# Graph attention layer: the own and row-aligned values are weighted and summed by GpSimd instead of VectorE

## The chip, the core and the metric

One core of a Trainium2 chip runs the kernel. The time is device microseconds of one execution. The engines of the core are TensorE (PE in the profile, PEld its weight loads), VectorE (DVE), ScalarE (ACT), GpSimd (POOL) and SyncE (SP); each works through its own instructions in the order in which they were written, and they wait for each other only by semaphores.

## What is computed

The reference is one layer of a graph network over 4096 nodes with 256 features, 8 heads of 32, all in float32; adj is a sparse matrix of 0 and 1.

```python
mask = adj.astype(jnp.float32) + jnp.eye(n, dtype=jnp.float32)
q = (h @ Wq.T + bq).reshape(n, N_HEADS, D_K)      # k, v in the same way
scores = jnp.einsum('nhd,mhd->hnm', q, k) / jnp.sqrt(jnp.float32(D_K))
scores = jnp.where(mask[None, :, :] == 0, jnp.float32(-1000000000.0), scores)
attn = jax.nn.softmax(scores, axis=-1)
ctx = jnp.einsum('hnm,mhd->nhd', attn, v).reshape(n, D_MODEL)
attn_out = ctx @ Wo.T + bo
h1 = _layer_norm(h + attn_out, ln1_g, ln1_b)
ff = jax.nn.relu(h1 @ W1.T + b1) @ W2.T + b2
return _layer_norm(h1 + ff, ln2_g, ln2_b)
```

## The kernel before

The kernel uses the sparsity. A first stage (up to about 100 us) projects keys, values and queries of all nodes and stores them as tables in device memory. VectorE searches each row of adj for its ones (`find_dve`, FIND_INDEX8 on L485), which gives lists of neighbours. A row of nodes sits on each of the 128 partitions; a tile is 128 nodes.

For each tile, keys and values come from three places: the node's own row (one plain load), the first one or two neighbours of each node (the row-aligned ones, gathered straight to the node's partition by GpSimd with indirect DMAs, L932), and the rest, the edges, packed into units of 128 and gathered by GpSimd (L940 for keys and values, L944 for queries). Own and aligned values are multiplied by their probabilities and added up elementwise; the edges are multiplied by theirs and then summed per node by TensorE with a one-hot matrix (`sum_pe`, L814), which adds the own sum in the same accumulation (L815).

The tiles after the first stage go in 19 steps, numbered 0 to 18 here. Steps 0 to 9 and 17, 18 hold two tiles, steps 10 to 16 one tile. Two tiles have 2 own slots each (own and one aligned), or 3 each in steps 6 to 9; a single tile has 3 own slots, or 4 in steps 14 and 15. Tile 0, with the most edges, is spread in pieces over steps 2 to 14. Two to four steps make a group of four tiles, and the dense part of a group (output projection L990, layer norm, feed-forward L1009 and L1021, second layer norm) is spread over the steps of the next group. The first step of a group is called place 0, the next place 1. The groups begin at steps 0, 2, 4, 6, 8, 10, 14 and 17.

The order of a step q on each engine is written out by hand. On VectorE: edge scores, own scores (`own_scores_dve`, whose reduction waits for `own_weighted` of the step before, since it overwrites the probabilities), mask and maximum, then the indices of the next step's edges (`cols_dve`, which lets GpSimd gather them), `norm_probs_dve` (ends with the own probabilities, semaphore `own_probs`), a search of a row tile for the step after next (one FIND_INDEX8 over 4105 elements for the two-tile steps), `edge_below_dve` (L651, after which ScalarE takes the exponential, L877), `own_sum_dve`, `edge_weight_dve` (L680, L683), a second search, the lists, and at place 0 the statistics of the second layer norm (L1075). On GpSimd: aligned gathers of the next step, four small operations of the first layer norm (`post_pool_rstd`) at place 0, edge gathers of the next step, at steps 2 to 8 two gathers for tile 0, then either gain and final of the output (L1102, L1106) at place 1 or the second `post_pool_rstd` at place 0. In steps 0 and 1, stores of query tiles (`store_q`, L1388) stand between them. TensorE's `sum_pe` waits for three semaphores: `edge_weighted`, `own_sum` and `own_weighted`. Behind it stand the dense matmuls of the step, and in steps 0 and 1 the last query projections. The aligned and edge gathers that reuse the buffers of step q wait for its `sum_pe` (semaphore `acc_ps`).

Of the kernel before, what the change touches and what calls it, by code (L numbers as in the profile page):

```python
# [5 lines left out]
ALU = mybir.AluOpType  # L6
# [6 lines left out]
P = 128  # L13
N = 4096
D = 256
HEADS = 8
DK = D // HEADS
# [97 lines left out]
def total(value, upto):  # L115

    return sum(value(q) for q in STEPS[:upto])
# [12 lines left out]
def build(nc, xT, adj, wqkvT, bq, bk, bqkv, woT, w1T, w2T, cols, g2, be2, out):  # L130
    with ExitStack() as ctx:
# [197 lines left out]
        own_probs = sem("own_probs")  # L329
# [70 lines left out]
        def wait(eng, s, value):  # L400
            if not isinstance(value, int) or value > 0:
                eng.wait_ge(s, value)
# [20 lines left out]
        def own_slots(q, ti):  # L423
            return slots[q.par][:, ti * q.own:(ti + 1) * q.own, :]
# [4 lines left out]
        def score_tiles(q):  # L429
            return scores[:, 0:q.T * q.S * HEADS].rearrange("p (t s h) -> p t s h", t=q.T, h=HEADS)  # L430

        def unit_scores(q, lo, hi):

            all_units = score_tiles(q)[:, :, 1:, :]
            if q.nu == 1:
                return all_units[:, :, lo:hi, :]
            return all_units[:, 0, :, :].rearrange("p (u r) h -> p u r h", r=q.room)[:, :, lo:hi, :]
# [213 lines left out]
            nc.vector.tensor_tensor(p_edge[:, 0:q.U, :], s_edge[:, 0:q.U, :], tr_out(q)[:, :, 0:HEADS], ALU.subtract  # L651
                                    ).then_inc(edge_below, 1)

        def own_sum_dve(dve, q):

            dve.wait_ge(own_probs, q.b + 1)
            for ti in range(q.T):
                v = own_slots(q, ti)[:, :, D:].rearrange("p s (h d) -> p s h d", d=DK)
                if q.nu == 1:
                    p = score_tiles(q)[:, ti, 0:q.own, :]  # L660
                    last = nc.vector.tensor_tensor(v, v, p.unsqueeze(3).to_broadcast([P, q.own, HEADS, DK]), ALU.mult)
                else:
                    p = score_tiles(q)[:, ti, 0:1, :]
                    last = nc.vector.tensor_tensor(v[:, 0:1], v[:, 0:1], p.unsqueeze(3).to_broadcast([P, 1, HEADS, DK]), ALU.mult)
                    if q.A:
                        p = unit_scores(q, 0, 1)[:, :, 0, :]
                        last = nc.vector.tensor_tensor(v[:, 1:], v[:, 1:], p.unsqueeze(3).to_broadcast([P, q.U, HEADS, DK]), ALU.mult)
            last.then_inc(own_weighted, 1)
            dve.wait_ge(own_weighted, q.b + 1)
            done = total(lambda p: p.own - 1, q.b)  # L670
            v = slots[q.par][:, 0:q.T * q.own, D:].rearrange("p (t s) d -> p t s d", s=q.own)
            for a in range(1, q.own):
                wait(dve, own_sum, done + a - 1)
                nc.vector.tensor_tensor(v[:, :, 0, :], v[:, :, 0, :], v[:, :, a, :], ALU.add).then_inc(own_sum, 1)  # L674

        def edge_weight_dve(dve, q):
            dve.wait_ge(edge_exp, q.b + 1)

# [217 lines left out]
        def ctx0_act(act):  # L896
            act.wait_ge(psum0, 2 * PIECES0 + 2)
            for k in range(KC):
                last = nc.scalar.activation(ctxT[:, k, TILE0.j * P:(TILE0.j + 1) * P], ps[:, ACC, k * 2 * P:(k * 2 + 1) * P], ACT.Identity,
                                            bias=bias_v[:, k:k + 1])  # L900
            last.then_inc(ctx0_ready, 1)

# [445 lines left out]
        def _(pool):  # L1350
# [49 lines left out]
            for q in STEPS:  # L1400
# [10 lines left out]
                    store_q(p)  # L1411
                if soon:
                    gather_edges(pool, soon)
                if 0 <= i - GATHER0 < PIECES0:
                    gather_edges(pool, TILE0, (2 * (i - GATHER0), 2 * (i - GATHER0) + 1))
                for gap in range(3, 5):
# [241 lines left out]
        def _(dve):  # L1658
# [43 lines left out]
            for q in STEPS:  # L1702
# [28 lines left out]
                if i == WEIGHTS0:  # L1731
                    edge_below0_dve(dve)
                edge_below_dve(dve, q)
                own_sum_dve(dve, q)
                edge_weight_dve(dve, q)
                if i == WEIGHTS0:
                    weight0_dve(dve, 0)
# [60 lines left out]
```

## Time and profile before

| | |
|---|---|
| median of 3 runs | 682.92 us |
| lowest, highest | 676.41, 685.6 us |
| the profiled execution's own time | 665.67 us |
| its span in the trace | 663.7 us |
| mean granted clock of TensorE | 0.903 |
| busy: TensorE, VectorE, GpSimd, ScalarE | 80%, 72%, 36%, 26% |

Busy shares are means over the span. The chain of waits is followed back from the last instruction, at each step to what released it, and tells which engine's work the end hung on at each time. A timeline row gives the start and the duration in us, and in brackets the idle time of that engine before it with what ended it. An indirect DMA on POOL is the time in which GpSimd issues it, not its transfer.

### The profile page before, as it was taken

To read this page: it belongs to the slowest core of one execution; us is meant where nothing else is said; L and a number is where in the kernel's file an instruction comes from. 1 tells how busy PE (TensorE), PEld (TensorE's weight loads), DVE (VectorE), ACT (ScalarE), POOL (GpSimd) and SP (SyncE) were. 2 spreads that over 40 slices of the span, in tenths; PEclk is the share of its full clock that TensorE was granted. 3 is DMA by queue.
4 is the path that set the end of the run, shared out by engine and by line. 5 is a ranking of instruction groups with operands and counts; after the bars stand their busy time and mean duration, and the time that the engine had idled before them with its cause. 6 is when DMAs were issued, how large, how long until landed. Compare 5 with 4: busy or idle time off the path is not lost.

```text
span 663.7 us, 7651 instructions
## 1 busy us (share of the span) xinstructions
PE 530.3 (80%) x2434; PEld 420.0 (63%) x2434; DVE 478.3 (72%) x1210; ACT 170.1 (26%) x357; POOL 238.9 (36%) x368
## 2 busy tenths in 40 slices
PE   6979679886797988789889785587858598989791
PEld 5868567775466748646775672366745368577680
DVE  1659687898885997999789798989985996412000
ACT  1111122212321341242224133111213213521610
POOL 5100033634331465446452434324351524122222
PEclk9989769989698999899789998678978889999896
DMA  9974689999886689686645527066672753020100
GB/s 332 409 302 161 230 309 327 406 347 339 325 285 229 217 317 336 200 341 239 253 134 207 206 58 259 19 244 244 223 236 66 262 182 110 18 64 0 33 16 19
DMA packets 39211, 141.08 MB, mean 213 GB/s; under 512 B 4856, under 2 KB 15352, under 8 KB 35072
## 3 DMA queue, kind: packets, MB, share of 16 engines
q1 hardware_dynamic: 24176, 94.90, 38.7%
q0 software_dynamic: 13328, 43.55, 19.2%
q10 hardware_dynamic: 1664, 2.11, 1.0%
q8 instruction: 21, 0.34, 0.2%
q14 instruction: 22, 0.18, 0.1%
HBM read 123.74 MB, written 16.80 MB: 212 GB/s over the span
## 4 chain that ended last, share of the span: by engine, by line
PE 43%; DVE 33%; issue 8%; DMA 7%; ACT 5%; POOL 3%; DVEq 0%; POOLq 0%; ACTq 0%
PE ps L1009 12%; PE ps L1021 10%; DVE found L485 8%; PE ps L990 4%; PE ps L980 3%; DMA adj_buf<-in_adj 3%; DVE stats L1075 2%; PE ps L1555 2%; PE ps L814 2%; PE ps L1573 2%; DMA work<-q_table,row_of 2%; PE ps L777 2%; DVE slots L674 2%; PE ps L815 1%; ACT early L1065 1%
## 5 line engine op out<-in xcount | busy, mean ns | idle before, releaser
L485 DVE FIND_INDEX8 found<-ones,adj_buf 128x8 uint32<-128x4105 int32 (+19 forms) x54 | 145.2, 2689 | 0.0
L1009 PE MATMUL ps<-xT_all,w 128*128 128x512 f32 (+1 forms) x288 | 129.5, 597 | 11.1 <-ACT xT_all L1055 10.0
L1021 PE MATMUL ps<-w,xT_all 128*128 128x256 f32 x512 | 121.9, 393 | 3.6 <-ACT xT_all L1055 2.7
L1021 PEld LDWEIGHTS ps<-w,xT_all 128*128 128x128 f32 x512 | 98.8, 198 | 17.7 <-ACT xT_all L1055 3.6
L1009 PEld LDWEIGHTS ps<-xT_all,w 128*128 128x128 f32 x288 | 57.2, 208 | 60.4 <-issue 45.4
L940 POOL DMA_INDIRECT slots<-kv_table,col_of x54 | 54.2, 1004 | 63.8 <-DVE col_of L558 52.2
L1075 DVE BATCH_NORM_STATS2 stats<-ps 128x6 f32<-128x256 f32 x64 | 22.9, 419 | 64.0 <-PE ps L980 64.0
L1555 PE MATMUL ps<-early,xT_all 128*128 128x256 f32 x256 | 63.6, 413 | 6.1 <-DMA early<-in_wqkvT 6.0
L1055 ACT ACTIVATE xT_all<-ps,col_table 128x512 f32<-128x512 f32 (+1 forms) x72 | 45.4, 642 | 71.5 <-PE ps L1009 65.7
L1555 PEld LDWEIGHTS ps<-early,xT_all 128*128 128x128 f32 x256 | 53.3, 210 | 14.8 <-DMA early<-in_wqkvT 6.0
L814 PE MATMUL ps<-work,slots 128*128 128x128 f32 x160 | 34.8, 327 | 28.8 <-DVE slots L683 28.8
L1093 POOL TENSOR_TENSOR rstd<-mv,eps_col 128x4 f32<-128x4 f32 (+1 forms) x18 | 5.4, 298 | 131.6 <-DVE mv L1081 131.6
L932 POOL DMA_INDIRECT slots<-kv_table,found x32 | 34.1, 1065 | 49.4 <-issue 23.2
L814 PEld LDWEIGHTS ps<-work,slots 128*128 128x128 f32 x160 | 28.1, 233 | 33.2 <-DVE slots L683 33.1
L990 PE MATMUL ps<-wo,xT_all 128*128 128x256 f32 x128 | 37.0, 415 | 14.3 <-issue 11.1
L944 POOL DMA_INDIRECT work<-q_table,row_of x40 | 39.2, 980 | 12.2 <-issue 12.2
L884 ACT ACTIVATE xT_all<-ps,col_table 128x256 f32<-128x256 f32 (+1 forms) x38 | 14.5, 431 | 109.4 <-PE ps L815 109.4
L1102 POOL TENSOR_TENSOR early<-early,row_g 128x1024 f32<-128x1024 f32 (+1 forms) x9 | 19.0, 2109 | 49.6 <-DVE slots L683 43.9
L1573 PE MATMUL ps<-early,xT_all 128*128 128x256 f32 x128 | 35.3, 401 | 0.0
L777 PE MATMUL ps<-idx_all,work 128*128 128x9 f32 (+1 forms) x80 | 12.7, 270 | 28.2 <-DVE work L539 28.2
L990 PEld LDWEIGHTS ps<-wo,xT_all 128*128 128x128 f32 x128 | 23.7, 206 | 16.9 <-issue 14.9
L777 PEld LDWEIGHTS ps<-idx_all,work 128*128 128x128 f32 x80 | 11.4, 206 | 32.6 <-DVE work L539 32.6
(160 smaller groups left out, 885.1 us busy)
## 6 DMA issues: line engine op xcount, KB each, us to landing
adj_buf<-in_adj SPq DMA_DIRECT2D x32, 2048.0 KB
xT_all<-in_xT SPq DMA_DIRECT2D x15, 512.0 KB, 22.0
kv_table<-slots POOLq DMA_DIRECT2D x7, 1024.0 KB, 5.0
slots<-kv_table SPq DMA_DIRECT2D x12, 512.0 KB
q_table<-slots POOLq DMA_DIRECT2D x16, 256.0 KB
out_dram<-early SPq DMA_DIRECT2D x7, 512.0 KB
q_own<-q_table SPq DMA_DIRECT2D x12, 256.0 KB
slots<-kv_table SPq DMA_DIRECT2D x8, 256.0 KB
```

The source lines that it names most:

```text
L485: last = nc.vector.max_index(dst, ones8[:], part)
L777: last = nc.tensor.matmul(lists_out(q)[:, u, :], rt[q.par][:, u, :], lists(q)[:, u, q.A:q.room + 2], start=True, stop=True)
L814: nc.tensor.matmul(to, edge_slots(q)[:, c, feats], onehot[q.par][:, c, :], start=(u == 0), stop=False)
L940: nc.gpsimd.indirect_dma_start(edge_slots(q)[:, u, :], None, kv_dram, bass.IndirectOffsetOnAxis(ap=col_of[q.par][:, u:u + 1], axis=0)).the ...
L944: nc.gpsimd.indirect_dma_start(q_edge[q.par][:, u, :], None, q_dram[q.no // 2], bass.IndirectOffsetOnAxis(ap=row_of[q.par][:, u:u + 1], ax ...
L990: nc.tensor.matmul(to, q["ctxT"][:, k, j * P:(j + 1) * P], wo[:, k, :], start=(k == 0), stop=False)
L1009: last = nc.tensor.matmul(ps[:, q["bank"] + f % 2, 0:q["g"] * P], w1[:, k, f * P:(f + 1) * P], q["h1T"][:, k, :], start=(k == 0), stop=(k ...
L1021: nc.tensor.matmul(to, q["ffT"][:, f, j * P:(j + 1) * P], w2[:, f, :], start=(f == 0), stop=False)
L1055: nc.scalar.activation(q["ffT"][:, f, :], ps[:, q["bank"] + f % 2, 0:q["g"] * P], ACT.Relu, bias=bias_1[:, f:f + 1]).then_inc(q["ff"], 1)
L1075: last = nc.vector.bn_stats(q["stats"][k][:, j, :], tile_out(q, q["bank"] + 2 * k, j))
L1555: last = nc.tensor.matmul(ps[:, kv_bank(i, part), j * D:(j + 1) * D], xT_all[:, c, k, r * P:(r + 1) * P], wqkv[:, k, (1 + part) * D:(2 + p ...
L1573: last = nc.tensor.matmul(to, xT_all[:, c, k, r * P:(r + 1) * P], wqkv[:, k, 0:D], start=False, stop=(k == KC - 1))
```

## The change

`own_sum_dve` is removed from VectorE and the same function is written for GpSimd: the multiplications of own and aligned values with their probabilities, and the additions. It stands in GpSimd's order behind the edge gathers of the next step and before the gathers for tile 0. Semaphores, tiles and the numbers of instructions stay the same. In the changed file L661, L664 and L667 of before are L890, L893 and L896, and L674 is L903.

```diff
@@ -651,28 +651,6 @@
             nc.vector.tensor_tensor(p_edge[:, 0:q.U, :], s_edge[:, 0:q.U, :], tr_out(q)[:, :, 0:HEADS], ALU.subtract
                                     ).then_inc(edge_below, 1)
 
-        def own_sum_dve(dve, q):
-
-            dve.wait_ge(own_probs, q.b + 1)
-            for ti in range(q.T):
-                v = own_slots(q, ti)[:, :, D:].rearrange("p s (h d) -> p s h d", d=DK)
-                if q.nu == 1:
-                    p = score_tiles(q)[:, ti, 0:q.own, :]
-                    last = nc.vector.tensor_tensor(v, v, p.unsqueeze(3).to_broadcast([P, q.own, HEADS, DK]), ALU.mult)
-                else:
-                    p = score_tiles(q)[:, ti, 0:1, :]
-                    last = nc.vector.tensor_tensor(v[:, 0:1], v[:, 0:1], p.unsqueeze(3).to_broadcast([P, 1, HEADS, DK]), ALU.mult)
-                    if q.A:
-                        p = unit_scores(q, 0, 1)[:, :, 0, :]
-                        last = nc.vector.tensor_tensor(v[:, 1:], v[:, 1:], p.unsqueeze(3).to_broadcast([P, q.U, HEADS, DK]), ALU.mult)
-            last.then_inc(own_weighted, 1)
-            dve.wait_ge(own_weighted, q.b + 1)
-            done = total(lambda p: p.own - 1, q.b)
-            v = slots[q.par][:, 0:q.T * q.own, D:].rearrange("p (t s) d -> p t s d", s=q.own)
-            for a in range(1, q.own):
-                wait(dve, own_sum, done + a - 1)
-                nc.vector.tensor_tensor(v[:, :, 0, :], v[:, :, 0, :], v[:, :, a, :], ALU.add).then_inc(own_sum, 1)
-
         def edge_weight_dve(dve, q):
             dve.wait_ge(edge_exp, q.b + 1)
 
@@ -899,6 +877,30 @@
                 last = nc.scalar.activation(ctxT[:, k, TILE0.j * P:(TILE0.j + 1) * P], ps[:, ACC, k * 2 * P:(k * 2 + 1) * P], ACT.Identity,
                                             bias=bias_v[:, k:k + 1])
             last.then_inc(ctx0_ready, 1)
+
+
+
+        def own_sum_pool(pool, q):
+
+            pool.wait_ge(own_probs, q.b + 1)
+            for ti in range(q.T):
+                v = own_slots(q, ti)[:, :, D:].rearrange("p s (h d) -> p s h d", d=DK)
+                if q.nu == 1:
+                    p = score_tiles(q)[:, ti, 0:q.own, :]
+                    last = nc.gpsimd.tensor_tensor(v, v, p.unsqueeze(3).to_broadcast([P, q.own, HEADS, DK]), ALU.mult)
+                else:
+                    p = score_tiles(q)[:, ti, 0:1, :]
+                    last = nc.gpsimd.tensor_tensor(v[:, 0:1], v[:, 0:1], p.unsqueeze(3).to_broadcast([P, 1, HEADS, DK]), ALU.mult)
+                    if q.A:
+                        p = unit_scores(q, 0, 1)[:, :, 0, :]
+                        last = nc.gpsimd.tensor_tensor(v[:, 1:], v[:, 1:], p.unsqueeze(3).to_broadcast([P, q.U, HEADS, DK]), ALU.mult)
+            last.then_inc(own_weighted, 1)
+            pool.wait_ge(own_weighted, q.b + 1)
+            done = total(lambda p: p.own - 1, q.b)
+            v = slots[q.par][:, 0:q.T * q.own, D:].rearrange("p (t s) d -> p t s d", s=q.own)
+            for a in range(1, q.own):
+                wait(pool, own_sum, done + a - 1)
+                nc.gpsimd.tensor_tensor(v[:, :, 0, :], v[:, :, 0, :], v[:, :, a, :], ALU.add).then_inc(own_sum, 1)
 
 
 
@@ -1411,6 +1413,7 @@
                     store_q(p)
                 if soon:
                     gather_edges(pool, soon)
+                own_sum_pool(pool, q)
                 if 0 <= i - GATHER0 < PIECES0:
                     gather_edges(pool, TILE0, (2 * (i - GATHER0), 2 * (i - GATHER0) + 1))
                 for gap in range(3, 5):
@@ -1731,7 +1734,6 @@
                 if i == WEIGHTS0:
                     edge_below0_dve(dve)
                 edge_below_dve(dve, q)
-                own_sum_dve(dve, q)
                 edge_weight_dve(dve, q)
                 if i == WEIGHTS0:
                     weight0_dve(dve, 0)
```

GpSimd, steps 0 and 1, from the edge gathers of step 0 for step 1. L1388 stores query tiles, L932 gathers aligned rows, L940 and L944 edges. Before:

```order
L940 DMA slots<-kv_table,col_of 128x512
L944 DMA work<-q_table,row_of 128x256
L1388 DMA q_table<-slots 128x2x256 x3
L932 DMA slots<-kv_table,found 128x512 x2
L1388 DMA q_table<-slots 128x2x256 x3
L940 DMA slots<-kv_table,col_of 128x512
L944 DMA work<-q_table,row_of 128x256
```

and now, two lines further down in the file:

```order
L942 DMA slots<-kv_table,col_of 128x512
L946 DMA work<-q_table,row_of 128x256
L890 TENSOR_TENSOR slots<-slots,scores 128x2x256 x2
L903 TENSOR_TENSOR slots<-slots 128x2x256
L1390 DMA q_table<-slots 128x2x256 x3
L934 DMA slots<-kv_table,found 128x512 x2
L1390 DMA q_table<-slots 128x2x256 x3
L942 DMA slots<-kv_table,col_of 128x512
```

The three elementwise instructions stand behind the last gather of step 0 and ahead of the stores.

VectorE, from the own probabilities (L640) of a two-tile step to its second search (MAX_INDEX is FIND_INDEX8 in the trace). Before:

```order
L640 TENSOR_TENSOR scores<-scores,top_rec 128x2x16
L485 MAX_INDEX found<-ones,adj_buf 128x8
L651 TENSOR_TENSOR p_edge<-s_edge,ps 128x16
L661 TENSOR_TENSOR slots<-slots,scores 128x2x256 x2
L674 TENSOR_TENSOR slots<-slots 128x2x256
L680 SCALAR_TENSOR_TENSOR p_edge<-p_edge,ps 128x16
L683 TENSOR_TENSOR slots<-slots,p_edge 128x2x256
L485 MAX_INDEX found<-ones,adj_buf 128x8
```

and now, where L658 and L661 are L680 and L683 of before:

```order
L640 TENSOR_TENSOR scores<-scores,top_rec 128x2x16
L485 MAX_INDEX found<-ones,adj_buf 128x8
L651 TENSOR_TENSOR p_edge<-s_edge,ps 128x16
L658 SCALAR_TENSOR_TENSOR p_edge<-p_edge,ps 128x16
L661 TENSOR_TENSOR slots<-slots,p_edge 128x2x256
L485 MAX_INDEX found<-ones,adj_buf 128x8
```

The weighting of the edges now follows the exponential of ScalarE directly.

## Rows read from the trace of the kernel before

**Rows 1.** The page, parts 1 and 4: busy time by engine; chain that ended last.
```profile
PE 530.3 (80%) x2434; PEld 420.0 (63%) x2434; DVE 478.3 (72%) x1210; ACT 170.1 (26%) x357; POOL 238.9 (36%) x368
...
PE 43%; DVE 33%; issue 8%; DMA 7%; ACT 5%; POOL 3%; DVEq 0%; POOLq 0%; ACTq 0%
```

**Rows 2.** VectorE by line: out<-in, count | busy us, mean ns | idle us before.
```profile
L674 DVE TENSOR_TENSOR slots<-slots 128x512 f32<-128x512 f32 (+1 forms) x32 | 17.9, 558 | 1.1
L661 DVE TENSOR_TENSOR slots<-slots,scores 128x512 f32<-128x512 f32 (+1 forms) x24 | 17.6, 774 | 0.0
```

**Rows 3.** GpSimd by line and form: busy us, mean ns | idle us before.
```profile
L1102 POOL TENSOR_TENSOR early<-early,row_g 128x1024 f32<-128x1024 f32 x7 | 16.5, 2351 | 45.9 <-DVE slots L683 43.9 <-ACT early L1065 2.0
L1102 POOL TENSOR_TENSOR early<-early,row_g 128x512 f32<-128x512 f32 x2 | 2.5, 1264 | 3.6 <-ACT early L1065 3.6
```

**Rows 4.** Timelines, step 4: start us, duration us, engine, line; in brackets idle before.
```profile
221.77 0.95 POOL L944 DMA_INDIRECT work<-q_table,row_of  x1 [0.30 <-issue]
223.21 1.29 DVE L661 TENSOR_TENSOR slots<-slots,scores 128x512 f32<-128x512 f32 x2
223.33 0.22 ACT L877 ACTIVATE p_edge<-p_edge 128x16 f32<-128x16 f32 x1 [4.18 <-issue]
225.34 0.69 DVE L683 TENSOR_TENSOR slots<-slots,p_edge 128x512 f32<-128x512 f32 x1
226.09 0.49 PE L814 MATMUL ps<-work,slots 128*128 128x128 f32 x2 [0.42 <-DVE slots L683]
```

**Rows 5.** Timelines of VectorE and GpSimd where instructions of both meet.
```profile
250.76 4.43 DVE L485 FIND_INDEX8 found<-ones,adj_buf 128x8 uint32<-128x4105 int32 x1
250.86 2.35 POOL L1102 TENSOR_TENSOR early<-early,row_g 128x1024 f32<-128x1024 f32 x1 [1.40 <-DVE slots L683]
424.81 2.35 POOL L1102 TENSOR_TENSOR early<-early,row_g 128x1024 f32<-128x1024 f32 x1 [13.88 <-DVE slots L683]
424.85 2.34 DVE L503 CAST aligned_idx<-idx_all 128x2 uint32<-128x2 f32 x1
```

**Rows 6.** Timelines of GpSimd and TensorE, steps 0 and 1.
```profile
123.00 0.38 PE L814 MATMUL ps<-work,slots 128*128 128x128 f32 x2
123.43 0.95 POOL L944 DMA_INDIRECT work<-q_table,row_of  x1 [0.30 <-issue]
146.04 0.49 PE L814 MATMUL ps<-work,slots 128*128 128x128 f32 x2 [0.32 <-DVE slots L683]
148.91 0.95 POOL L944 DMA_INDIRECT work<-q_table,row_of  x1 [0.30 <-issue]
152.68 1.10 PE L990 MATMUL ps<-wo,xT_all 128*128 128x256 f32 x4 [1.20 <-ACT xT_all L1029]
```

**Rows 7.** Timelines of GpSimd and TensorE, steps 2, 8, 11, 14, 17.
```profile
166.91 0.95 POOL L944 DMA_INDIRECT work<-q_table,row_of  x1 [0.30 <-issue]
170.88 0.80 PE L814 MATMUL ps<-work,slots 128*128 128x128 f32 x2 [4.56 <-DVE slots L683]
334.46 0.95 POOL L944 DMA_INDIRECT work<-q_table,row_of  x1 [0.30 <-issue]
340.35 0.80 PE L814 MATMUL ps<-work,slots 128*128 128x128 f32 x2 [2.09 <-DVE slots L683]
424.78 1.22 PE L814 MATMUL ps<-work,slots 128*128 128x128 f32 x4 [6.44 <-DVE slots L683]
487.36 1.66 POOL L944 DMA_INDIRECT work<-q_table,row_of  x1 [0.30 <-issue]
490.71 1.65 PE L814 MATMUL ps<-work,slots 128*128 128x128 f32 x6 [7.10 <-DVE slots L683]
563.17 0.95 POOL L944 DMA_INDIRECT work<-q_table,row_of  x1 [0.30 <-issue]
565.00 0.39 PE L814 MATMUL ps<-work,slots 128*128 128x128 f32 x2
```

**Rows 8.** Window 160 to 180: busy us of PE, PEld, DVE, ACT, POOL; granted clock; DMA.
```profile
160.00:180.00 20.00, 12.01 (x40) 8.63 (x41) 18.53 (x44) 6.21 (x13) 10.08 (x12) 0.66 0.87 303
```

## The prediction

> **What bounds the kernel now.** I read the shares of the page first, then its chain of waits, then timelines of single steps. VectorE is busy 478.3 us (72%), GpSimd 238.9 us (36%), TensorE 530.3 us [rows 1], which alone would speak for moving work from VectorE to GpSimd. The chain says that the end hangs on TensorE for 43% and on VectorE for 33% of the span [rows 1], by turns: in a place-0 step TensorE ends up waiting for VectorE, in a place-1 step its feed-forward matmuls set the pace. So the question in each step is which of three things `sum_pe` gets last: the weighted edges from VectorE, the own sum, or TensorE's own time.
>
> **What VectorE loses.** L661 is 24 instructions, 17.6 us, L674 32 instructions, 17.9 us [rows 2]; L664 and L667 are the multiplications of the single tiles. In a two-tile step with one aligned neighbour, L661 starts at 223.21 and the edge weighting L683 at 225.34, ending at 226.03 [rows 4]: 2.0 us of own sum lie between. They also covered ScalarE's exponential (223.33, 0.22 us [rows 4]), after which L680 can run. So the weighting can now start at about 223.75 and the gain is some 1.5 us per step where VectorE is the last, not 2.0; with three slots (steps 6 to 9) some 2.7.
>
> **What GpSimd gains.** A tensor_tensor of two inputs takes 2.351 us for 1024 elements per partition and 1.264 for 512 [rows 3], so 2.12 ns per element and 0.18 us fixed: 0.72 us for 256, 1.81 for 768. A two-tile step then costs 3 x 1.264 = 3.8 us (two multiplications, one addition), with three slots 2 x 1.81 + 2 x 1.264 = 6.15, a single tile 0.72 + 1.264 + 2 x 0.72 = 3.4, with four slots 0.72 + 1.81 + 3 x 0.72 = 4.7, each plus 0.1 to 0.3 for semaphores. The trace shows the operand of these rows repeated over rows, not over single elements of a head as here, and rows of 256 inside a pitch of 512. Bounds: VectorE's own time for the same work (two thirds less wait), or twice the rows; I take the rows.
>
> **Where it stands.** The whole first search (4.43 us [rows 5]) lies between the own probabilities and L661, so those are ready before GpSimd comes to them in nearly every step. What sets the start is the end of the edge gathers of the next step in front. In step 4 the last of them ends at 222.72 [rows 4], so the own sum ends at 226.6 where `sum_pe` started at 226.09 [rows 4]. Behind it on GpSimd wait tile 0's gathers (used two steps later), the second `post_pool_rstd` or gain and final, and then aligned gathers; none of them has less than about 1 us of room except where named below.
>
> **The two engines meet.** At 424.85 a CAST of 128x2 elements on VectorE lasts 2.34 us, exactly to the end of GpSimd's L1102, begun at 424.81; while a FIND_INDEX8 keeps its 4.43 us beside the same operation at 250.86 [rows 5]. So some instructions of VectorE stand still for a whole GpSimd operation. L683, with two inputs in SBUF, never meets one in this trace. Its price is between nothing and all multiplications of the step (2.5 us, 3.6 with three slots). I take the one that runs when it arrives, up to 1.3 us, and let GpSimd wait 0.69 us for L683 in turn. That leaves 0.8 of the 1.5 us of gain in step 4, and puts `sum_pe` 1.2 us later there, which its later work hides (the chain leaves the step by the statistics of the second layer norm).
> [...]
>
> **Step by step, on the path:**
> - Steps 0 and 1, the largest term. In step 0 the last gather ends at 124.38 and `sum_pe` started at 123.00 [rows 6], so it waits to 128.3, 5.3 us later. Behind it are two query projections, whose copies stand in ScalarE's queue before the distances of step 2; part of this has slack, and I take 2.5 us for step 1. There the last gather ends at 149.86, behind stores of queries, while `sum_pe` started at 146.04 [rows 6]. The own sum ends at 149.86 + 2.5 + 3.8 = 156.2, so `sum_pe` comes 10.2 us later, and with it the last query projection, its copy, the biasing of x on ScalarE and the output projection at 152.68 [rows 6]. I take 0.7 us off as an allowance for room further down: **+9.5**.
> - Step 2: last gather ends 167.86, own sum with one collision 172.4, `sum_pe` was at 170.88 after a wait of 4.56 [rows 7]: +1.6. Step 13 repeats it: **+3.2** together.
> - Step 8: 335.41 + 6.15 + 0.2 + 0.7 = 342.5 against 340.35 [rows 7]: **+2.3** (step 6 has the same pattern, but ScalarE's queue hides it: 0).
> - Step 14: 489.02 + 4.7 + 0.3 = 494.0 against 490.71 [rows 7]: **+3.3**.
> - Step 17: 564.12 + 3.8 + 0.2 = 568.1 against 565.00 [rows 7]: **+3.1**.
> - Step 11: the gathers are long done; `sum_pe` at 424.78 had waited 6.44 for VectorE [rows 7], now 1.5 less. The same in step 12; 0.9 in step 10, 0.8 in step 4: **-4.7**. Step 15: 0.
> - Place 1 (steps 3, 5, 7, 9, 16) and step 18: TensorE arrives at `sum_pe` after the own sum; 0. Cover: the feed-forward matmuls. Were they gone, each would cost 2 to 4 us.
> - TensorE's clock: after the wait of 4.56 us its first pair of `sum_pe` takes 0.80 us against 0.38 without a wait [rows 6, 7], and the granted clock of that stretch is 0.66 [rows 8], so part of it at 1.2 instead of 2.4 GHz. The new waits in steps 0 and 1 should bring one or two such stretches. Estimate from these rows, between 0 and 5: **+2**.
>
> Sum: 9.5 + 3.2 + 2.3 + 3.3 + 3.1 - 4.7 + 2 = 18.7, say +19 us on the profiled execution's 665.67 (span 663.7), so 685 for a profile like that one. It lies 17 us below the median of the runs shown, 682.92, to which I add the same: **702 us**, 2.8% slower.
>
> **Rivals.**
> - The early delay is hidden. If ScalarE's and TensorE's work in steps 0 and 1 closes up again (query projections are filler, nothing of the path is in them), or GpSimd's operations are a third cheaper, then 9.5 shrinks to 0 to 3 and the clock term goes: +8 to +10, about 692. For it: TensorE is busy but not late there. Against it: the output projection needs the context of step 1, and started 1.20 us after TensorE had nothing else to do [rows 6].
> - VectorE's relief decides: faster. If the own sum ends before L683 does wherever VectorE is last, each of the ten steps 2, 4, 6, 8 and 10 to 15 gives 1.5 (six two-slot or single-tile ones), 2.7 (two) or 2.1 (two): 9 + 5.4 + 4.2 = 18.6 less, about 664. The point from which it decides: the gathers' end plus the GpSimd sum before VectorE's new end of L683; at step 4 that is 226.6 against 224.5, so GpSimd's price would have to fall from 3.8 to 1.8 us, below anything in rows 3.
> - The collision is dear. GpSimd's instructions follow each other without a gap in which L683 could enter, so it is held for all multiplications, and the small list operations behind it as well: 1.3 us more in each of seven place-0 steps, +9, about 712.
> - The change does not do what it says: the order lists show the instructions moved in all 19 steps, so no chance.
>
> **Chances.** Forecast 0.60 (its own range 692 to 711), hidden early delay 0.22, relief 0.06, dear collision 0.12. A measurement of this kernel tells 2% (14 us) from no change. Of the forecast's chance a tenth falls short of 2%; with the second case this makes 0.27 for within 2%, 0.05 faster, 0.68 slower. The range takes in the hidden delay from below and most of the dear collision: 686 to 714.
>
> **What would show it.** In the changed profile: TensorE's L814 waits for POOL at the additions (now L903) in steps 0, 1, 2, 8, 13, 14 and 17, the longest in step 1, near 8 us or more; the output projection after step 1 starts near 163; a GpSimd tensor_tensor of 512 takes 1.26 us; VectorE's edge weighting comes right after L658, or stretched to the end of a GpSimd multiplication. It would be wrong if GpSimd's instruction takes under 1 us or over 2 for 512 elements, or if the first feed-forward of the first group starts less than 4 us later than before.

## The result

| | before | changed |
|---|---|---|
| median, same chip | 679.66 us (675.88 to 685.6, 4 runs) | 688.09 us (686.92 to 691.74, 4 runs) |
| ratio | | 1.025, 95% interval 1.019 to 1.031 |
| the profiled execution's own time | 665.67 us | 688.35 us |
| span, granted clock | 663.7 us, 0.903 | 686.0 us, 0.886 |

The change makes the kernel 2.5% slower, some 17 us. The kernel before has executions that take over 1.5% longer than its fastest, and the ratio leaves such slow ones out, which is why it isn't the quotient of the two medians (1.012). The two profiled executions lie 22 us apart, which is more than that. A second profile of the kernel before (an experiment below) has 675.56 us; the difference to it is 12.8 us, and the interval of the ratio, 13 to 21 us, reaches to it. Differences between traces in what follows are against this second profile. They are single executions: the two profiles of the unchanged kernel lie 9.9 us apart in span (663.7 and 673.6), and the shift between them changes by up to 2.4 us from one step to the next after step 1. A difference of 1 or 2 us at one step is therefore a reading and not a proof.

The page of the changed kernel, busy time by engine and the chain that ended last (before: [rows 1]):

```profile
PE 536.4 (78%) x2434; PEld 425.7 (62%) x2434; DVE 473.0 (69%) x1140; ACT 169.6 (25%) x357; POOL 312.0 (45%) x438
PE 40%; DVE 28%; POOL 10%; DMA 8%; issue 7%; ACT 5%; POOLq 0%; DVEq 0%; ACTq 0%
```

GpSimd has 73 us more work. VectorE lost 70 instructions and yet is only 5 us less busy. The chain passes through GpSimd for 10% of the span, before 3%.

GpSimd's moved instructions in the changed kernel, by line and form (before: [rows 2] on VectorE, [rows 3] for the price assumed); count, busy us, mean ns:

```profile
L890 POOL TENSOR_TENSOR slots<-slots,scores 128x512 f32<-128x512 f32 x16 | 16.4, 1053 | 11.8 <-DVE scores L640 11.7
L890 POOL TENSOR_TENSOR slots<-slots,scores 128x768 f32<-128x768 f32 x8 | 11.7, 1492 | 0.1
L903 POOL TENSOR_TENSOR slots<-slots 128x512 f32<-128x512 f32 x16 | 23.1, 1443 | 1.3
```

Multiplications take 1.05 us for 512 elements and 1.49 for 768, less than the 1.264 and 1.81 assumed; the addition takes 1.44 in the mean, 1.26 to 1.30 where it meets no edge weighting and 1.60 in step 2 (below). VectorE in the same kernel, three lines that were not touched:

```profile
L661 DVE TENSOR_TENSOR slots<-slots,p_edge 128x512 f32<-128x512 f32 x17 | 20.5, 1204 | 0.6
L497 DVE CAST idx_all<-found 128x16 f32<-128x16 uint32 x12 | 10.3, 857 | 0.4
L510 DVE TENSOR_TENSOR mask<-idx_all,limit 128x16 f32<-128x16 f32 x17 | 7.7, 456 | 0.4
```

The edge weighting took 692 ns and takes 1204; the CAST took 243 and takes 857. All removed instructions of VectorE had 43.7 us; the groups that stay have grown by 34.7 us together: 9.3 the edge weighting and 24.9 the list operations (CAST, L518, L510, L500, L525). That is where most of VectorE's relief went.

Not all of it is held by the own sum. Two of the four long CASTs end with GpSimd's L1104, the gain of the output, which before ran beside the search (it began at 315.81 in step 7) and now comes later:

```profile
328.20 2.84 DVE L497 CAST idx_all<-found 128x16 f32<-128x16 uint32 x1
328.63 2.36 POOL L1104 TENSOR_TENSOR early<-early,row_g 128x1024 f32<-128x1024 f32 x1
```

So the own sum also costs VectorE by pushing GpSimd's other work from the search, which isn't held, onto instructions that are.

TensorE's waits for the own sum, us in total, times, longest:

```profile
PE ps L792 <- POOL slots L903: 40.6, 8, 9.3
```

Timelines of steps 0 and 1 in the changed kernel (start us, duration us; [rows 6] is the same place before):

```profile
122.34 0.95 POOL L946 DMA_INDIRECT work<-q_table,row_of  x1 [0.30 <-issue]
123.31 2.06 POOL L890 TENSOR_TENSOR slots<-slots,scores 128x512 f32<-128x512 f32 x2
125.44 1.30 POOL L903 TENSOR_TENSOR slots<-slots 128x512 f32<-128x512 f32 x1
126.84 0.46 PE L792 MATMUL ps<-work,slots 128*128 128x128 f32 x2 [4.67 <-POOL slots L903]
155.99 0.94 POOL L946 DMA_INDIRECT work<-q_table,row_of  x1 [0.30 <-issue]
156.38 2.67 DVE L497 CAST idx_all<-found 128x16 f32<-128x16 uint32 x1
156.95 2.06 POOL L890 TENSOR_TENSOR slots<-slots,scores 128x512 f32<-128x512 f32 x2
159.09 1.30 POOL L903 TENSOR_TENSOR slots<-slots 128x512 f32<-128x512 f32 x1
160.49 0.77 PE L792 MATMUL ps<-work,slots 128*128 128x128 f32 x2 [7.26 <-POOL slots L903]
169.22 1.10 PE L992 MATMUL ps<-wo,xT_all 128*128 128x256 f32 x4 [1.88 <-ACT xT_all L1031]
```

The order is as predicted: last gather, own sum, `sum_pe`. In step 1 GpSimd reaches the own sum at 156.95, `sum_pe` starts at 160.49 after a wait of 7.26 us, and the output projection at 169.22, 10.3 us later than in the second profile of before (158.93), which is the forecast difference (163 against 152.68). The first feed-forward of the first group starts 9.4 us later (191.22 against 181.82). A CAST of VectorE lasts 2.67 us here, to the end of GpSimd's multiplications at 159.01.

Step 2, where the edge weighting meets GpSimd (before: [rows 7], first pair):

```profile
183.84 2.05 POOL L890 TENSOR_TENSOR slots<-slots,scores 128x512 f32<-128x512 f32 x2
184.54 1.91 DVE L661 TENSOR_TENSOR slots<-slots,p_edge 128x512 f32<-128x512 f32 x1
185.97 1.60 POOL L903 TENSOR_TENSOR slots<-slots 128x512 f32<-128x512 f32 x1
187.67 0.77 PE L792 MATMUL ps<-work,slots 128*128 128x128 f32 x2 [5.39 <-POOL slots L903]
```

The edge weighting starts at 184.54 and ends 0.56 us after the multiplications of GpSimd do (185.89). It came during the first of them, was not let in between the two, and takes 1.2 us longer than its 0.69. The same 0.55 to 0.56 us stand between these two ends in steps 3 to 9, where it comes just before the end of the first or during the second, and takes 0.4 to 1.5 us longer. GpSimd's addition takes 1.60 us here and 1.30 where it meets no edge weighting (step 1), so it is held in turn, but by 0.3 us and not the 0.69 that was assumed.

Step 14 (before: [rows 7]), and then the starts of `sum_pe` in steps 11 and 12:

```profile
507.27 0.94 POOL L946 DMA_INDIRECT work<-q_table,row_of  x1 [0.30 <-issue]
508.80 1.49 POOL L896 TENSOR_TENSOR slots<-slots,scores 128x768 f32<-128x768 f32 x1
510.37 2.35 POOL L903 TENSOR_TENSOR slots<-slots 128x256 f32<-128x256 f32 x3
512.82 1.62 PE L792 MATMUL ps<-work,slots 128*128 128x128 f32 x6 [9.29 <-POOL slots L903]
```

```profile
440.81 1.23 PE L792 MATMUL ps<-work,slots 128*128 128x128 f32 x4 [4.51 <-DVE slots L661]
467.30 0.61 PE L792 MATMUL ps<-work,slots 128*128 128x128 f32 x4
```

In step 14 the own sum sets the start. In step 11 VectorE is still last, but the wait has gone from 6.44 to 4.51 us. In step 12 TensorE comes straight from its feed-forward, without a wait. `sum_pe` waits for GpSimd in steps 0, 1, 2, 6, 8, 14, 15 and 17: all that the prediction named but step 13, and steps 6 (3.12 us) and 15 (5.61 us), which it had priced at nothing. The longest wait is that of step 14, not of step 1.

### The profile page after: what moved, and what is told of

Same layout as the page of the kernel before. It is cut to its first block, busy times and chain, and to the rows that moved or that the text cites. A ratio compares the mean times of both kernels' runs of the same rounds, so it can differ in the third digit from the quotient of the medians.

```text
span 686.0 us, 7651 instructions
## 1 busy us (share of the span) xinstructions
PE 536.4 (78%) x2434; PEld 425.7 (62%) x2434; DVE 473.0 (69%) x1140; ACT 169.6 (25%) x357; POOL 312.0 (45%) x438
## 3 DMA queue, kind: packets, MB, share of 16 engines
q0 software_dynamic: 13328, 43.55, 18.7%
## 4 chain that ended last, share of the span: by engine, by line
PE 40%; DVE 28%; POOL 10%; DMA 8%; issue 7%; ACT 5%; POOLq 0%; DVEq 0%; ACTq 0%
PE ps L1011 12%; PE ps L1023 10%; DVE found L485 8%; PE ps L992 4%; PE ps L982 3%; DMA q_table<-slots 3%; DMA adj_buf<-in_adj 3%; PE ps L792 3%; POOL slots L942 2%; PE ps L1558 2%; DVE stats L1077 2%; DMA work<-q_table,row_of 2%; POOL work L946 2%; PE ps L793 2%; POOL slots L903 2%
## 5 line engine op out<-in xcount | busy, mean ns | idle before, releaser
L1011 PE MATMUL ps<-xT_all,w 128*128 128x512 f32 (+1 forms) x288 | 131.7, 605 | 7.1 <-ACT xT_all L1057 6.0
L1023 PE MATMUL ps<-w,xT_all 128*128 128x256 f32 x512 | 126.4, 403 | 3.6 <-ACT xT_all L1057 3.1
L1023 PEld LDWEIGHTS ps<-w,xT_all 128*128 128x128 f32 x512 | 102.0, 204 | 19.0 <-ACT xT_all L1057 4.1
L942 POOL DMA_INDIRECT slots<-kv_table,col_of x54 | 52.0, 963 | 66.4 <-DVE col_of L558 55.9
L792 PE MATMUL ps<-work,slots 128*128 128x128 f32 x160 | 37.5, 347 | 48.6 <-POOL slots L903 40.6
L1558 PE MATMUL ps<-early,xT_all 128*128 128x256 f32 x256 | 60.8, 401 | 6.3 <-DMA early<-in_wqkvT 6.3
L792 PEld LDWEIGHTS ps<-work,slots 128*128 128x128 f32 x160 | 30.5, 251 | 53.1 <-issue 47.1
L992 PE MATMUL ps<-wo,xT_all 128*128 128x256 f32 x128 | 34.8, 396 | 14.6 <-issue 8.9
L903 POOL TENSOR_TENSOR slots<-slots 128x512 f32<-128x512 f32 (+1 forms) x32 | 37.7, 1178 | 2.5
L1576 PE MATMUL ps<-early,xT_all 128*128 128x256 f32 x128 | 35.9, 406 | 0.0
L890 POOL TENSOR_TENSOR slots<-slots,scores 128x512 f32<-128x512 f32 (+1 forms) x24 | 28.2, 1200 | 11.9 <-DVE scores L640 11.7
```

Source lines behind the costliest of these rows:

```text
L792: nc.tensor.matmul(to, edge_slots(q)[:, c, feats], onehot[q.par][:, c, :], start=(u == 0), stop=False)
L903: nc.gpsimd.tensor_tensor(v[:, :, 0, :], v[:, :, 0, :], v[:, :, a, :], ALU.add).then_inc(own_sum, 1)
L942: nc.gpsimd.indirect_dma_start(edge_slots(q)[:, u, :], None, kv_dram, bass.IndirectOffsetOnAxis(ap=col_of[q.par][:, u:u + 1], axis=0)).the ...
L992: nc.tensor.matmul(to, q["ctxT"][:, k, j * P:(j + 1) * P], wo[:, k, :], start=(k == 0), stop=False)
L1011: last = nc.tensor.matmul(ps[:, q["bank"] + f % 2, 0:q["g"] * P], w1[:, k, f * P:(f + 1) * P], q["h1T"][:, k, :], start=(k == 0), stop=(k ...
L1023: nc.tensor.matmul(to, q["ffT"][:, f, j * P:(j + 1) * P], w2[:, f, :], start=(f == 0), stop=False)
```

## The experiments

Each kernel is compared with the kernel before on the same chip. Late steps are 2 to 18, early ones 0 and 1.

### The kernel before once more, profiled a second time

No edit.

> The kernel before, unchanged, profiled once more. In the first profile of before the edge gather that VectorE waits for in step 1 landed at 130.2 us, in the changed kernel and in the three variants run so far at 136. If this is a matter of the execution and not of the change, it lands near 136 here, the span is near 669 us, and the effect of the change on the trace is about 17 us, not 22. If the change delays it, it lands at 130 again. Time: the same as before, ratio 0.995 to 1.005 on either account.

Measured: 673.86 us, ratio 0.998 (0.993 to 1.002). Rows of the second profile of before, timelines of steps 0 and 1:

```profile
123.48 0.39 PE L814 MATMUL ps<-work,slots 128*128 128x128 f32 x2
123.92 0.94 POOL L944 DMA_INDIRECT work<-q_table,row_of  x1 [0.30 <-issue]
135.88 0.69 DVE L575 TENSOR_TENSOR work<-work,slots 128x512 f32<-128x512 f32 x1 [7.83 <-DMA work<-q_table,row_of]
152.29 0.49 PE L814 MATMUL ps<-work,slots 128*128 128x128 f32 x2 [0.31 <-DVE slots L683]
155.16 0.95 POOL L944 DMA_INDIRECT work<-q_table,row_of  x1 [0.30 <-issue]
158.93 1.88 PE L990 MATMUL ps<-wo,xT_all 128*128 128x256 f32 x4 [1.21 <-ACT xT_all L1029]
```

VectorE's first edge operation of step 1 (L575) starts at 135.88, in the first profile it started at 130.22; in the changed kernel at 136.06. The gather that it waits for was issued at 123.92, 123.43 and, in the changed kernel, 122.34. So the transfer is not later by the change, and 5.7 us of the 22 between the two first profiles are a matter of the execution at this place; at the end it is 9.9 us. The expectation was right for the transfer, and for the span too low (669 expected, 673.6 measured). Waits of the same kernel, for comparison below:

```profile
PE ps L814 <- DVE slots L683: 27.3, 7, 7.1
DVE work L575 <- DMA work<-q_table,row_of: 17.1, 4, 7.8
```

### Only the late steps, only the early steps

```diff
+ON_POOL = set(range(2, NB))     # late;  {0, 1} in early and early_again
...
-                own_sum_pool(pool, q)
+                if q.b in ON_POOL:
+                    own_sum_pool(pool, q)
...
                 edge_below_dve(dve, q)
+                if q.b not in ON_POOL:
+                    own_sum_dve(dve, q)
```

> Own sum on VectorE again in steps 0 and 1, on GpSimd in steps 2 to 18. Queue theory (TensorE's summing matmuls wait for GpSimd, and most of the loss comes where query stores and gathers stand in front, steps 0 and 1): 16 to 17 us of the 22 come back, so +4 to +9 us against before, ratio about 1.01. Collision rival (the loss comes from instructions of VectorE and GpSimd that block each other, spread over all steps): 17 of 19 steps still collide, so +17 to +21 us.

> The own sum on GpSimd in steps 0 and 1 alone, on VectorE in the other 17. Queue theory: +13 to +17 us against before. Collision rival: +2 to +4.

> GpSimd has the own sum in steps 0 and 1 alone, VectorE in all others; the same kernel as the earlier one with only the early steps moved, whose four times lay between 679 and 693 us. The prediction's largest term says +9.5 us from these two steps: ratio to before 1.010 to 1.018, and in the profile the statistics and the edges of steps 3 to 8 come 8 to 10 us later than in the second profile of before. Rival (early delay hidden): below 1.005, and the delay shrinks to under 4 us by step 5.

Measured: late 684.07 us, ratio 1.017 (1.012 to 1.022). Early gave 679.3, 690.4, 692.8 and 692.9 us, too scattered for a ratio. Its second run gave 682.58 us, ratio 1.009 (1.004 to 1.013). The first two starts of `sum_pe` in the second run of the early steps, and that of step 3:

```profile
127.13 0.77 PE L815 MATMUL ps<-work,slots 128*128 128x128 f32 x2 [4.68 <-POOL slots L926]
159.39 0.77 PE L815 MATMUL ps<-work,slots 128*128 128x128 f32 x2 [7.26 <-POOL slots L926]
212.84 0.39 PE L815 MATMUL ps<-work,slots 128*128 128x128 f32 x2
```

Against 123.48 and 152.29 before these are 3.6 and 7.1 us later, and step 3 (206.11 before) 6.7. From there the difference is between 6.6 and 6.8 us at every edge step and at the end, so nothing takes it back. The 8 to 10 us expected were too many, and the ratio is just under the 1.010 expected, with an interval that reaches over it. The late steps end 6.3 us behind in their profile, inside the 4 to 9 expected; their ratio, some 12 us, lies between that and the 17 to 21 of the collision rival. The parts add up: 6.6 + 6.3 = 12.9 us against 12.4 for the last instruction of the changed kernel, and 0.9% + 1.7% against 2.5% in the timed runs. That the traces agree so well is partly chance, since executions differ by more; the timed ratios and the waits for GpSimd (4.68 and 7.26 us, none for it in the kernel before) carry the reading. "Early delay hidden" is out: it allowed a ratio below 1.005 and under 4 us by step 5.

### Own sum cut to one element, on GpSimd and on VectorE

The instructions and their semaphores stay, each on 128x1 elements; the weighting and sum of own and aligned values are thereby left out.

```diff
-nc.gpsimd.tensor_tensor(v, v, p.unsqueeze(3).to_broadcast([P, q.own, HEADS, DK]), ALU.mult)
+nc.gpsimd.tensor_tensor(v[:, 0, 0, 0:1], v[:, 0, 0, 0:1], p[:, 0, 0:1], ALU.mult)
...
```

> As the changed kernel, with every instruction of the own sum on GpSimd cut to one element per partition (the rest of the weighting and the sum is left out), at the same places and with the same waits: what is left is the place in GpSimd's queue and the relief of VectorE. Queue theory: steps 0 and 1 still cost 4 to 6 us since the gathers stand in front, elsewhere the sum is ready before the weighted edges, and VectorE's relief (some 1.5 to 2.7 us a step where it is last) counts in full: -5 to -12 us against before. If GpSimd's duration did not matter, about +15 or more. Collision rival: nothing blocks VectorE any more, -12 to -18.

> The own sum on VectorE as before, every instruction of it cut to one element per partition (the rest of the weighting and the sum is left out): the bound of what relieving VectorE could give. Relief theory and queue theory alike: -8 to -16 us against before. It is lower than the kernel with the small instructions on GpSimd by what their place in GpSimd's queue costs, 4 to 6 us by the queue theory, 0 to 2 by the collision rival.

Measured: on GpSimd 662.23 us, ratio 0.984 (0.977 to 0.991); on VectorE 658.06 us, ratio 0.979 (0.973 to 0.986). TensorE's waits for GpSimd in the first:

```profile
PE ps L815 <- POOL slots L926: 12.8, 4, 6.0
```

So VectorE's relief is worth 14 us (2.1%) where nothing takes its place, and the rival "relief decides" had 18.6. Both kernels lie inside what was expected of them. Standing behind the gathers alone costs some 3 us of it, by ratios whose intervals overlap; that it costs something is shown by the 12.8 us of waits for GpSimd. The queue theory had 4 to 6 us and the collision rival 0 to 2.

### Fills in place of the arithmetic

```diff
-last = nc.gpsimd.tensor_tensor(v, v, p..., ALU.mult)
+last = nc.gpsimd.memset(own_slots(q, ti), 0.001)
...
-nc.gpsimd.tensor_tensor(v[:, :, 0, :], v[:, :, 0, :], v[:, :, a, :], ALU.add)
+nc.gpsimd.memset(slots[q.par]...[:, :, 0, :], 0.001 * a)
```

> The changed kernel with its multiplications and additions on GpSimd replaced by fills of the same places in the queue, which read no SBUF and are sized for about 1 us each; the own values are thereby not weighted, so this part of the computation is left out. Queue theory: position and duration stay, so sum_pe waits as in the changed kernel, ratio 1.015 to 1.025, while VectorE's L661 keeps its 0.69 and 0.96 us. Collision rival: without reads nothing holds VectorE, ratio 1.005 or less.

Measured: 679.86 us, ratio 1.009 (1.005 to 1.013): between the two expectations. GpSimd's fills, and VectorE's two lines with them:

```profile
L913 POOL MEMSET slots<- 128x1024 f32 x16 | 14.9, 969 | 11.1 <-DVE scores L641 11.1
L926 POOL MEMSET slots<- 128x1024 f32 x16 | 15.2, 951 | 0.9
```

```profile
L684 DVE TENSOR_TENSOR slots<-slots,p_edge 128x512 f32<-128x512 f32 x17 | 11.8, 692 | 0.6
L498 DVE CAST idx_all<-found 128x16 f32<-128x16 uint32 x12 | 10.4, 869 | 0.4
```

The same lines in the second profile of before:

```profile
L683 DVE TENSOR_TENSOR slots<-slots,p_edge 128x512 f32<-128x512 f32 x17 | 11.8, 692 | 0.6
L497 DVE CAST idx_all<-found 128x16 f32<-128x16 uint32 x12 | 2.9, 243 | 0.4
```

Two places of the fill kernel's timelines:

```profile
154.92 2.44 DVE L498 CAST idx_all<-found 128x16 f32<-128x16 uint32 x1
155.47 1.86 POOL L913 MEMSET slots<- 128x1024 f32 x2
181.57 1.88 POOL L913 MEMSET slots<- 128x1024 f32 x2
182.30 0.69 DVE L684 TENSOR_TENSOR slots<-slots,p_edge 128x512 f32<-128x512 f32 x1
```

The edge weighting keeps 692 ns; it runs 0.69 us from 182.30 in the middle of two fills, and keeps its own duration in all steps where it meets one. But the CAST is held by the fills (2.44 us, to their end at 157.33), which I had not expected: "without reads nothing holds VectorE" was wrong. It began 0.55 us before the first fill, while GpSimd was still issuing a gather, and would have been done before the fill otherwise (0.17 us in most places), so that issue seems to hold it too; this was not tested by itself. Its mean of 869 ns is not all due to fills: of its five long instances two end with fills and three with GpSimd's output arithmetic (L1127, L1131). So there are two kinds of meeting in these traces: the multiplication with two inputs in SBUF waits for a GpSimd instruction that reads and not for a fill, the CAST for both.

The Trainium skill (SBUF — State Buffer, "Who interferes with whom") says that a VectorE instruction with two SBUF inputs contends with a GpSimd one that reads SBUF and not with one that only writes, and that VectorE's two-port modes do contend; the first half agrees with the 0.69 us beside a fill and the 1.91 beside a multiplication, the second with the CAST if that runs in such a mode, which no run here shows by itself.

The fills are also shorter by 0.5 us in a two-tile step (1.88 + 0.95 against 2.06 + 1.30), so the 11 us between this kernel and the changed one are not the holding alone. And holding is not gone here: VectorE's instructions together are still 19 us longer than the same ones before, against 34.7 in the changed kernel.

### The own sum ahead of the gathers

```diff
+                if q.b in AHEAD:         # all 19 steps;  all but 0, 1, 13, 14, 17
+                    own_sum_pool(pool, q)
                 if soon:
                     gather_edges(pool, soon)
-                own_sum_pool(pool, q)
```

In the second of the two the steps named have it on VectorE.

> The same GpSimd instructions in all 19 steps, but placed ahead of the next step's edge gathers. Queue theory (the end of the gathers in front sets when the own sum ends, and so the loss): the own sum ends before the search does, sum_pe no longer waits for it, and in the steps in which VectorE waits for the edge gathers (1, 14, 15, 18) these come 3.4 to 6 us later, so part of the gain is given back: ratio to before 0.985 to 1.01. Collision rival (VectorE's edge weighting, stretched by GpSimd, is what costs): the additions and multiplications now run beside the search, which is not held, so 0.98 to 0.99. Rival that moving the work cannot pay because GpSimd's operations are slow wherever they stand: 1.015 or more.

> As the version with the own sum ahead of the gathers, but steps 0, 1, 13, 14 and 17 have it on VectorE as before, since there the gathers are the later. Queue theory: what the gathers lose is gone, VectorE's relief stays in the other steps: 0.98 to 0.99 of before (bound: the 0.979 of the kernel in which the own sum is next to nothing). Collision rival: the same or a little less. Slow wherever they stand: 1.0 or above.

Measured: all steps 700.29 us, ratio 1.034 (1.026 to 1.043); the picked ones 687.13 us, ratio 1.017 (1.011 to 1.022). Both expectations of the queue theory were wrong, and so were those of the collision rival: the edge weighting is back at 0.69 us in most steps of the first, and its ratio is the largest of all. By the numbers alone "slow wherever they stand" fits both. The waits give another cause, and the next experiment, in which GpSimd has the own sum in 11 steps and nothing is lost, speaks against that rival. VectorE's waits in the first:

```profile
DVE work L577 <- DMA work<-q_table,row_of: 84.9, 14, 10.8
```

The 17.1 us in 4 steps of the kernel before have become 84.9 in 14. Step 4, with the gathers for step 5:

```profile
236.02 2.05 POOL L914 TENSOR_TENSOR slots<-slots,scores 128x512 f32<-128x512 f32 x2 [1.38 <-DVE scores L642]
239.59 1.04 POOL L966 DMA_INDIRECT slots<-kv_table,col_of  x1 [0.16 <-issue]
243.44 0.95 POOL L970 DMA_INDIRECT work<-q_table,row_of  x1 [0.30 <-issue]
255.84 0.69 DVE L577 TENSOR_TENSOR work<-work,slots 128x512 f32<-128x512 f32 x1 [6.44 <-DMA work<-q_table,row_of]
```

The own sum holds GpSimd from 236.02 to 239.42, the last query gather is issued at 243.44, and VectorE gets it 12.4 us later, after waiting 6.44. The delay of some 3.4 us and more shows in 14 steps, so in most of them these transfers had less room than that. I had taken the four steps with a wait in the trace for the only ones without room. So the place ahead of the gathers is no better than the one behind them (1.034 against 1.025, with intervals that overlap).

### Only the steps that the prediction priced at nothing or as a gain

```diff
+ON_POOL = {3, 4, 5, 7, 9, 10, 11, 12, 15, 16, 18}
```

> GpSimd has the own sum only in the 11 steps that the prediction priced at nothing or as a gain: 3, 4, 5, 7, 9, 10, 11, 12, 15, 16 and 18. By the prediction's terms -4.7 us or 0.993; by what the changed kernel's profile showed of these steps (gain in 11 lost again in 12, edge weighting stretched by 0.1 to 1.2 us in nearly all) nothing: 0.997 to 1.003. Rival that each GpSimd operation costs through collisions wherever it stands: 1.005 or more.

Measured: 661.8, 664.3, 672.4 and 672.6 us, ratio 0.982 (0.977 to 0.987), which rests on the first two. The profiled execution is one of the other two and 2.9 us under the second profile of before (672.62 against 675.56). By both it isn't slower; between 0.4% and 1.8% of gain stays open, where the prediction's terms said 0.7% and my later expectation nothing. So the loss sits in the other eight steps, 0, 1, 2, 6, 8, 13, 14 and 17, of which the prediction had named all but step 6 as the places of loss (step 6, priced at nothing, was left out here since `sum_pe` waited 3.12 us for GpSimd there in the changed kernel).

### The additions on TensorE

VectorE multiplies as before, but no longer adds; TensorE accumulates each own slot with the identity, ahead of its wait for the edges.

```diff
+            for ti in range(q.T):
+                for k in range(KC):
+                    for a in range(q.own):
+                        nc.tensor.matmul(to, own_slots(q, ti)[:, a, feats], ident[:], ...)
+            pe.wait_ge(edge_weighted, q.b + 1)
             for ti in range(q.T):
...
-                    last = nc.tensor.matmul(to, own_slots(q, ti)[:, 0, feats], ident[:], ...)
```

> GpSimd has nothing of it. VectorE multiplies the own values in all steps, but in the steps 0, 2, 4, 6, 8, 10, 11, 12, 14 and 17 the addition is left to TensorE, which accumulates the own slots one by one ahead of its wait for the weighted edges. VectorE loses 0.69 us (two-tile) to 0.85 or 1.3 us (three slots) in each, and TensorE's four to eight further multiplications of 0.22 us run while it waits anyway. Theory that in these steps VectorE is what sum_pe waits for: 0.6 to 1.3 us gained in each, ratio 0.988 to 0.997. Rival that TensorE is as short of time there: 1.00 or above.

> The addition left to TensorE in all 19 steps. In the other nine steps TensorE comes last to sum_pe by its own time, so 4 to 12 further multiplications of 0.22 us each lengthen it by 0.9 to 1.8 us where VectorE's relief is worth nothing: 5 to 10 us above the version with only the ten steps, ratio 0.995 to 1.01.

Measured: in ten steps 669.42 us, ratio 0.990 (0.985 to 0.995); in all 19 steps 668.41 us, ratio 0.991 (0.986 to 0.996). The first lies inside what was expected. Both take about 1% less than the kernel before, and so 3.4% less than the changed one. That the other nine steps would cost 5 to 10 us was wrong: the two can't be told apart. The page and the `sum_pe` line of the version with ten steps:

```profile
PE 541.0 (82%) x2534; PEld 432.8 (65%) x2534; DVE 469.8 (71%) x1193; ACT 169.8 (26%) x357; POOL 239.9 (36%) x368
L831 PE MATMUL ps<-work,slots 128*128 128x128 f32 x160 | 26.4, 291 | 4.0 <-DVE slots L688 4.0
```

TensorE's 100 further multiplications cost 3 us of busy time, and its wait for the weighted edges fell from 27.3 us to 4.0. Another 12.1 us, in 3 waits, now stand before its multiplications of the own slots.

## Why the prediction was right, and where not

The direction, the mechanism and most of the size were right: 2.5%, where 2.8% was forecast. The time itself was forecast worse than the difference. 688 us is 14 below the 702, because the 19 us were added to a median of 682.92, while a ratio of 1.025 puts 688 some 17 us above a kernel before of 671. It lies outside the forecast's own range (692 to 711) and inside the full one only by the part that was added for the hidden early delay, which the experiments rule out; that was luck. Point by point, "at `sum_pe`" being the start of its first multiplication against the second profile of before (the shift is 8.8 us in step 7, 10.1 in 8, 11.4 in 9 and 10, 9.7 in 11, 11.4 in 12, 12.5 in 13, 14.8 in 14, 13.1 in 15, 12.8 in 16, 15.0 in 17):

| term | predicted | measured |
|---|---|---|
| steps 0 and 1 | +9.5 | +8.2 at `sum_pe` of step 1; +6.6 at the end with these steps alone |
| steps 2 and 13 | +3.2 | 1.2 and 1.1 more at `sum_pe` |
| step 8 | +2.3 | +1.3 at `sum_pe` of step 8, +2.6 by that of step 9 (the prediction's own figures give 2.15, not 2.3) |
| step 14 | +3.3 | +2.3 at `sum_pe`, +0.6 left in step 15 |
| step 17 | +3.1 | +2.2 at `sum_pe`, not seen at the end (12.4) |
| steps 4, 10, 11, 12 | -4.7 | -0.7 by step 5, nothing in 10, -1.7 in 11, given back in 12 |
| TensorE's clock | +2 | none seen: mean 0.886 against 0.882 |
| sum | +18.7 | +12.4 in the trace, some +17 timed |

- **Steps 0 and 1** were the largest term and are. The term was mis-sized by 1 to 3 us: GpSimd takes 3.4 us instead of 3.8, and of the 2.5 us carried from step 0 to step 1 only 0.8 arrived: the last gather of step 1 ended at 156.93 against 156.11.
- **The gains** failed in the changed kernel. The trace shows little of the 4.7 us. In step 12 VectorE was credited with 1.5 us, but TensorE comes to `sum_pe` by its own feed-forward once VectorE is earlier. The wait in [rows 7] was read for step 11 and carried over to step 12. How that goes with the 0.4 to 1.8% gained in the 11 steps alone stays open. With them the collision was undersized, though not for L683: up to 1.3 us was taken for it, and 0.4 to 1.5 us in a step is what it lost, 9.3 in all. What was left out are the list operations behind it (CAST, L518, L510, L500, L525), 24.9 of the 34.7 us. That is the mechanism of the rival "collision is dear". It cost no 9 us on top; a likely reason, not tested, is that most of those instructions lie off the path, as in steps 2, 6 and 8, where `sum_pe` waits for GpSimd's addition, which ends after L683.
- **The clock** term isn't seen in the means. In step 1 `sum_pe` does run slower after its new wait (0.77 us for the first pair, 0.49 in the second profile of before), and from 120 to 130 us, around the new wait of step 0, the granted clock is 0.87 instead of 1.00. But from 100 to 200 us together it is 0.85 against 0.86.
- **The sum** came out close partly by offset: the gains were too large by some 4 us, the costs of steps 0 and 1 and of the clock together by 3 to 5, and those of steps 14 and 17, 6.4 us, leave hardly 1 us at the end of the trace.
- **"Relief decides"** had the value of the relief nearly right (18.6, measured 14), and the condition that it names is not met: GpSimd would have had to fall to 1.8 us and took 3.4.

What the stack of kernels says, each as a share of before: relief of VectorE -2.1%, standing in GpSimd's queue +0.4%, the time on GpSimd +2.6%, and reads and longer operations +1.6%; together +2.5%. Each part is the difference of two ratios, each known to half a percent or so, and not all of them were timed on the same chip. The fill kernel holds VectorE's small copies as well, so the third part contains some holding. How much of it was not separated.

## What to carry to other kernels

Moving work from the busier engine to an idle one pays only where the new engine delivers before the last input that the consumer waits for; price each step by the end of the queue in front plus the operation, not by shares, and move it only in the steps that have room: in 11 of the 19 the same move gained 0.4 to 1.8% here. If the two engines hold each other, count the relief as given back instruction by instruction, small ones included, and ask which of the new engine's other work is pushed beside them. Where the consumer itself waits idle, let it do the work while it waits: the additions on TensorE gained 1% where the whole own sum on GpSimd lost 2.5%.

## What was not expected of the hardware

- On GpSimd the multiplication with a repeated operand takes 1.05 us for 512 elements, the addition of two full operands in rows of 256 takes 1.26 to 1.30 where it meets no edge weighting; both write 512 elements per partition.
- A CAST of 128x16 elements on VectorE, 0.24 us in the mean before, took up to 2.84 us beside GpSimd's arithmetic and up to 2.44 us beside GpSimd fills that read nothing, while a multiplication of 128x512 elements passed such fills in its usual 0.69 us.
- One and the same kernel used a gathered transfer at 130.22 us in one execution and at 135.88 in another, though it was issued at 123.43 and 123.92. The gap never closed; at the end of the traces it was 9.9 us.
